# The second expert loop starts while attention still runs: four pairs of expert tiles between the steps of the last turn and the routing

## The reference

```
x = x + 0.5 * ffn(layernorm(x))
x = x + attention(layernorm(x))
x = x + 0.5 * ffn(layernorm(x))
```

```
p = softmax(xt @ Wr + br);  probs, idx = top_k(p, 2);  probs /= probs.sum
h = layernorm(relu(xt @ W1[e] + b1[e]))        # 128 -> 512
y = layernorm(relu(h @ W2[e] + b2[e]))         # 512 -> 128
out = sum over the two chosen experts of probs * y
```

## Time and profile before

| | |
|---|---|
| time, median of 3 runs | 481.54 us (480.0, 481.54, 481.68) |
| profiled execution, from the first instruction to the last | 480.5 us |
| mean granted clock of TensorE | 0.987 of full speed |
| TensorE busy | 430.7 us, with filler |
| VectorE busy | 351.1 us |
| ScalarE busy | 293.5 us |
| GpSimd busy | 244.9 us |

### The profile page before, as it was taken

The page is one execution under the profiler, slowest core; times in us unless marked ns, Lnnn a source line. Parts: engine busy times, 40 slices in busy tenths (PEclk is TensorE's granted clock), DMA queues, the critical chain, the costliest instruction groups (busy, mean ns, idle before and its releaser), DMA issues.

```text
span 480.5 us, 12115 instructions
## 1 busy us (share of the span) xinstructions
PE 430.7 (90%) x3768; PEld 288.1 (60%) x3769; DVE 351.1 (73%) x1268; ACT 293.5 (61%) x593; POOL 244.9 (51%) x344
## 2 busy tenths in 40 slices
PE   7999999999999977889988889878789999999994
PEld 7653676777765444556555565544436777777743
DVE  5874778787886287868889898764654878878764
ACT  1495776666665155777877878747215666676640
POOL 8684634334401557474765847658431454555440
PEclk9997999999999999999999999999999999999999
DMA  7900144445431110000000001101111111111017
GB/s 233 347 25 28 33 137 144 143 154 198 148 123 66 34 34 22 25 13 12 25 24 24 12 25 37 33 23 40 34 51 45 44 51 56 55 52 48 33 49 243
DMA packets 25855, 35.09 MB, mean 73 GB/s; under 512 B 4282, under 2 KB 18546, under 8 KB 24659
## 3 DMA queue, kind: packets, MB, share of 16 engines
q1 hardware_dynamic: 20866, 24.62, 15.4%
q0 software_dynamic: 4944, 9.90, 7.2%
HBM read 15.45 MB, written 18.24 MB: 70 GB/s over the span
## 4 chain that ended last, share of the span: by engine, by line
DVE 32%; PE 28%; issue 12%; ACT 12%; DMA 6%; POOL 5%; DVEq 4%; SPq 1%; POOLq 0%; ACTq 0%
ACT wide L641 8%; DVE st L1037 6%; DVE mx L1649 4%; DVE yy L1054 3%; DMA yk<-y_scratch,posi 3%; DVE st L1060 3%; DVE yy L1058 2%; PE bank L1409 2%; PE bank L1919 2%; POOL yk L1184 2%; DVEq L1054 2%; PE bank L1470 2%; DVE mv L1065 2%; DMA early<-y_scratch 2%; PE bank L1552 2%
## 5 line engine op out<-in xcount | busy, mean ns | idle before, releaser
L807 PEld LDWEIGHTS bank<-w2c,hT 128*128 128x128 f32 x624 | 74.2, 191 | 24.4 <-issue 23.8
L807 PE MATMUL bank<-w2c,hT 128*128 x624 | 76.7, 276 | 3.4 <-ACT hT L663 1.7
L789 PE MATMUL bank<-w1s,xT 128*128 x156 | 73.8, 594 | 0.6 <-DVE w2c L1805 0.6
L1649 DVE TENSOR_REDUCE mx<-bank 128x4 f32<-128x1024 f32 (+1 forms) x48 | 58.4, 1220 | 10.0 <-PE bank L1440 10.0
L412 POOL DMA_INDIRECT y_scratch<-yo,dest_u x39 | 39.2, 1006 | 50.0 <-ACT yo L656 43.7
L1285 ACT ACTIVATE early<-bank 128x768 f32<-128x768 f32 x64 | 51.9, 814 | 20.5 <-PE bank L1460 20.1
L422 POOL DMA_INDIRECT xgw<-xn_scratch,slot_u x39 | 37.2, 953 | 53.2 <-PE bank L781 44.0
L1037 DVE BATCH_NORM_STATS2 st<-wide 128x6 f32<-128x512 f32 x78 | 50.2, 685 | 17.2 <-ACT wide L641 15.8
L663 ACT COPY hT<-bank 128x1024 f32<-128x1024 f32 (+1 forms) x40 | 39.6, 990 | 24.2 <-PE bank L798 24.2
L798 PE MATMUL bank<-ident,wide 128*128 128x128 f32 x312 | 42.0, 277 | 6.5 <-ACT wide L641 6.4
L1184 POOL DMA_INDIRECT yk<-y_scratch,posi x32 | 31.8, 992 | 22.9 <-issue 6.6
(11 more groups left out here) (341 smaller groups left out, 912.1 us busy)
## 6 DMA issues: line engine op xcount, KB each, us to landing
xr_scratch<-row_buf SPq DMA_DIRECT2D x8, 1032.0 KB, 4.1
xgw<-xr_scratch SPq DMA_DIRECT2D x39, 64.5 KB, 1.8
y_scratch<-yo SPq DMA_DIRECT2D x19, 128.0 KB, 1.8
w1s<-in_L_ffn_W_dram SPq DMA_DIRECT2D x1, 2048.0 KB, 9.7
early<-y_scratch SPq DMA_DIRECT2D x8, 256.0 KB, 3.8
xn_scratch<-row_buf SPq DMA_DIRECT2D x1, 1024.0 KB, 5.1
out_dram<-xs SPq DMA_DIRECT2D x8, 128.0 KB, 2.3
row_buf<-row_buf SPq DMA_DIRECT2D x6, 128.0 KB, 2.2
```

Of the source, the lines that this page charges most:

```text
L789: last = pe.matmul(bank[1 + 2 * u + j][:], xT[:, u, j, :], w1s[:, bass.ds(e * FF, FF)], start=True, stop=True)
L807: last = pe.matmul(bank[7][:, j * DIM:(j + 1) * DIM], hT[:, u, j, c * P:(c + 1) * P], w2c[:, bass.ds(e * (FC * DIM) + c * DIM, DIM)], star ...
L1649: dve.tensor_reduce(mx[:, c:c + 2 * per].rearrange("p (a q) -> p q a", q=2), quad[:, low:low + 2, :].rearrange("p q (a e) -> p q a e", a=p ...
```

## The change

The first four pairs of f2 no longer stand in or ahead of the loop. They are written out by hand among the steps of what was turn 10 and the routing of batches 6 and 7. The attention pipeline now ends after turn 9, and its last steps (D of batch 7) stand in this section. For this there are three tile tables in place of one (`tile_table(..., q)`): the first, in turn 9, gives 8 tiles filled from the rows of batches 0 to 3; the second gives 12 from batches 0 to 6; the third the other 19. A table takes only tiles that are full, and carries what it used to the next (`used`, `stride`, `first_at`). `load_tiles` waits for the table and for the scatters of its own row tiles. The filler between these steps is gone, and so are two loads of ScalarE's function table: the exponential of the gates is a power on GpSimd behind the fifth outgoing pair. `gates`, its transpose (`turn_gates`) and its copy (`gates_turned`) stand between the loop and the last four pairs. Within f2 the hidden products of all pairs use one pair of banks (3, 4), so `hidden(m)` waits for relu of m-1.

```diff
+AHEAD = 4
+TABLES = (0, 2 * AHEAD, 20, SLOT_TILES)
...
+            for q in range(3):
+                load_tiles(sp, S, q)
...
+        def load_tiles(sp, S, q):
+            a, b = TABLES[q], TABLES[q + 1]
+            where = lambda n: sp.value_load(addr[0:1, n:n + 1], min_val=0, max_val=(NE * TT + NE - 2) * P)
+            sp.wait_ge(S["slot"], q + 1)
+            first = [where(n) for n in range(a, a + 4)]
+            sp.wait_ge(*scattered(q))
+            for n in range(a, b):
+                p = n // 2
+                v = first[n - a] if n < a + 4 else where(n)
+                if p >= 2:
+                    sp.wait_ge(S["xTp"], p - 1)
+                    sp.wait_ge(S["dest"], p - 1)
+                sp.dma_start(xgw[:, n % 4, :], xr_dram[bass.ds(v, P), :]).then_inc(S[f"xg{n % 4}"], 16)
+        SCATTERED_BY = (0, 8, 14, TT)
+        def scattered(q):
+            semaphore, rows_before = (first_row(0, 0), first_row(0, 1), (sems["f2"]["sc"], 0))[q]
+            return semaphore, rows_before + 16 * TOPK * (SCATTERED_BY[q + 1] - SCATTERED_BY[q])
...
+                pool.wait_ge(S["base"], 3)
+                numbers(0)
+                numbers(1)
+                scatter(pool, S, 12)
+                scatter(pool, S, 13)
+                numbers(2)
+                outgoing(0)
+                numbers(3)
+                scatter(pool, S, 14)
+                scatter(pool, S, 15)
+                numbers(4)
+                for p in range(1, PAIRS):
+                    outgoing(p)
                     if p + 4 < PAIRS:
                         numbers(p + 4)
+                    if p == 4:
+                        pool.wait_ge(S["top"], 1)
+                        pool.tensor_tensor(gden[:], euler[:], mw[:], ALU.pow).then_inc(S["gexp"], 1)
...
+        def pair_banks(S):
+            return (bank[0], (1, 3)) if S is sems["f1"] else (bank[2], (3, 3))
...
-                turn_batch(pe, S, BATCH - 1)
-                keep_warm(1, 6)
-                batch_logits(pe, S, BATCH - 1)
-                keep_warm(4, 6)
-                batch_ranks(pe, S, BATCH - 1)
-                pe.wait_ge(S["base"], 7)
-                pe.matmul(bank[5][:, 0:NE], ones16[:], picks[:, BATCH, 0, :], start=True, stop=True).then_inc(S["rankp"], 1)
-                keep_warm(30, 6)
...
+                if h_at[0] == h_at[1]:
+                    if not (isinstance(m, int) and m == 0):
+                        pe.wait_ge(S["relu"], m)
...
+            def turn_gates():
+                pe.wait_ge(S["gsum"], 1)
+                pe.transpose(gates_bank(first), gsum[:], ident[:]).then_inc(S["gTp"], 1)
...
+                step.settle()
             step(dve.tensor_scalar(one(ntile_i), one(ntile_i), 7, None, ALU.arith_shift_right))
-            step(dve.tensor_tensor(one(ntile), one(ntile_i), picks[0:1, 0, 0, :], ALU.subtract))
+            step(dve.tensor_tensor(one(ntile), one(ntile_i), used[:, 0:NE], ALU.subtract))
+            step.begin(dve.tensor_tensor(stride[:], stride[:], one(ntile), ALU.subtract))
             step(dve.tensor_tensor(one(tri), one(e_lt), ntile[0:1, None, :].to_broadcast([1, NE, NE]), ALU.mult))
...
+            shape = [1, n, NE]
+            step(dve.tensor_tensor(ecmp[:, 0:n], tile_iota[0:1, 0:n, None].to_broadcast(shape), end[0:1, None, :].to_broadcast(shape), ALU.is_ge))
+            step.begin(dve.tensor_reduce(eidf[:, a:b], ecmp[:, 0:n], X, ALU.add))
+            gaps = ecmp[:, 24:24 + n]
+            step(dve.tensor_tensor(gaps, ecmp[:, 0:n], stride[:, None, :].to_broadcast(shape), ALU.mult))
+            begun = lg[0:1].rearrange("p a b -> p (a b)")[:, 0:n]
+            step(dve.tensor_reduce(begun, gaps, X, ALU.add))
+            dve.scalar_tensor_tensor(addr[:, a:b], begun, float(P), first_at[:, 0:n], ALU.mult, ALU.add).then_inc(S["slot"], 1)
+            pack_experts(dve, S, step, a, b)
+            if final:
+                dve.tensor_tensor(mw[:], best8[:, :, 1], best8[:, :, 0], ALU.subtract).then_inc(S["top"], 1)
+                return
+            step(dve.tensor_scalar(one(start), one(start), float(n), None, ALU.min))
+            step(dve.scalar_tensor_tensor(one(end), one(end), float(n), one(start), ALU.min, ALU.subtract))
+            step(dve.tensor_tensor(used[:, 0:NE], used[:, 0:NE], one(end), ALU.add))
+            dve.wait_ge(S["slot"], q + 1)
+            step.begin(dve.tensor_tensor(stride[:], used[:, 1:NE + 1], used[:, 0:NE], ALU.subtract))
+            step(dve.tensor_scalar(first_at[:], tile_iota[0:1, 0:40], used[:, 0:1], float(P), ALU.add, ALU.mult))
...
-            with dve.Fori(1, PAIRS // 2 - 2) as i:
...
+            with dve.Fori(1 if first else AHEAD // 2, PAIRS // 2 - 2) as i:
...
+            if not first:
+                gates(dve, S, step)
...
+            d = BATCH - 1
+            act.activation(spad, eps_c[:], ACT.Sqrt)
+            deviations(act, F, d - 1)
+            half_values(1, d)
+            relu(0, 0)
+            copy_xT(1, 1)
+            turned_batch(act, F, d - 1)
+            copy_hT(0, 0)
+            squares(d)
+            relu(1, 1)
+            act.wait_ge(A["msq"], BATCH)
+            act.activation(orr[:], oms[:], ACT.Sqrt).then_inc(A["rms"], 1)
+            sqrt1(0, 0)
+            copy_xT(2, 0)
+            outputs_turned(d, bank[1])
+            copy_hT(1, 1)
+            relu(2, 0)
+            deviations(act, F, d)
+            sqrt2(0, 0)
+            sqrt1(1, 1)
+            turned_batch(act, F, d)
+            finish(0, 0)
+            copy_xT(3, 1)
+            copy_hT(2, 0)
+            relu(3, 1)
+            sqrt2(1, 1)
+            sqrt1(2, 0)
+            finish(1, 1)
+            copy_hT(3, 1)
+            copy_xT(4, 0)
+            sqrt1(3, 1)
+            sqrt2(2, 0)
+            relu(4, 0)
+            copy_xT(5, 1)
+            finish(2, 0)
...
+            d, e = BATCH - 1, experts(pe, eid, 0, 2 * AHEAD)
+            hidden(0, 0, e[0:2])
+            turn_values(d)
+            pe.wait_ge(A["x2"], d)
+            turn_batch(pe, F, d - 1)
+            turn_x(1, 0, 1)
+            turn_h(0, 0)
+            pe.wait_ge(A["ow"], d + 1)
+            batch_logits(pe, F, d - 1)
+            hidden(1, 1, e[2:4])
+            pe.wait_ge(F["xnTc"], d)
+            second(0, 0, e[0:2])
+            turn_outputs(d, bank[1])
+            batch_ranks(pe, F, d - 1)
+            turn_h(1, 1)
+            turn_x(2, 1, 0)
+            output_products(d, bank[1])
+            hidden(2, 0, e[4:6])
+            second(1, 1, e[2:4])
+            turn_batch(pe, F, d)
+            turn_x(3, 1, 1)
+            turn_h(2, 0)
+            batch_logits(pe, F, d)
+            hidden(3, 1, e[6:8])
+            second(2, 0, e[4:6])
+            batch_ranks(pe, F, d)
+            turn_h(3, 1)
+            pe.wait_ge(F["eid"], 2)
+            later = experts(pe, eid, 2 * AHEAD, 2)
+            turn_x(4, 2, 0)
+            second(3, 1, e[6:8])
+            hidden(4, 0, later)
+            turn_x(5, 2, 1)
...
+                if t == BATCH + 1:
+                    tile_table(dve, F, step, 0)
...
+            d, e = BATCH - 1, experts(dve, eid, 0, 2 * AHEAD - 2)
+            d_step.start(d * D_STEPS)
+            dve.wait_ge(A["x2"], d)
+            row_stats(dve, F, 2 * d - 2, 2 * d)
+            late_norm(dve, F, step, d - 1)
+            weigh(d)
+            outputs(d)
+            stats1(0, 0)
+            mean_squares(d)
+            batch_best(dve, F, step, d - 1)
+            batch_places(dve, F, step, d - 1)
+            rms(d)
+            moments1(0, 0)
+            batch_marks(dve, F, step, d - 1)
+            batch_slots(dve, F, step, d - 1)
+            stats1(1, 1)
+            residual(d, bank[1])
             dve.wait_ge(A["x2"], BATCH)
+            row_stats(dve, F, 2 * d, TT)
+            y_part(0, 0, e[0:2])
+            late_norm(dve, F, step, d)
+            y_norm(0, 0, e[0:2])
+            moments1(1, 1)
+            tile_table(dve, F, step, 1)
+            batch_best(dve, F, step, d)
+            batch_places(dve, F, step, d)
+            batch_marks(dve, F, step, d)
+            y_part(1, 1, e[2:4])
+            batch_slots(dve, F, step, d)
+            stats1(2, 0)
+            y_norm(1, 1, e[2:4])
+            moments1(2, 0)
+            tile_table(dve, F, step, 2)
+            stats1(3, 1)
+            y_part(2, 0, e[4:6])
+            moments1(3, 1)
+            y_norm(2, 0, e[4:6])
+            stats1(4, 0)

```

More of the change, by code:

```diff
@@ L811, in body @@
+            if first:
+                turn_gates()
+            pe.wait_ge(S["eid"], 1 if first else 3)
+            turn_x, hidden, turn_h, second = tensor_pair(pe, S)
             def body(n, i, u, e, kx=2, kh=2, k=2):
@@ L1165, in turns @@
         def turns(eng, turn):
-            for t in range(BATCH + 3):
+            for t in range(BATCH + 2):
                 turn(t, t % 2)
@@ L1532, in turn @@
                         turn8(k6, 0, bank[2][:]).then_inc(A["kTp"], 1)
```

(3 more changed lines are left out.)

411 lines of the change are left out of this document (197 added, 214 removed).

## The result

The changed kernel takes 486.06 us (median of 8 runs, 483.64 to 488.94), the kernel before 482.53 on the same chip (8 runs, 480.00 to 484.11): a ratio of 1.0074, 95% interval 1.0045 to 1.0103. It is slower, by 3.5 us, where 480.1 was predicted, with a range of 475.8 to 484.0. The profiled execution of the changed kernel has a span of 481.9 us and a run time of 483.64, the shortest of the eight.

A forecast was written before the change was run, and what follows sets the result against it. VectorE with ScalarE was taken to bound the loop, behind a single chain across engines. 6.6 us gained before the loop, less 2.5 at the gates and 2.7 for the clock, gave 480.1 us from 481.5; range 475.8 to 484.0.

The forecast's parts named there:

- Tables of 3.9, 3.9 and 3.5 us: VectorE's three new tile tables: forecast working times, with bounds of 3.4 and 4.5 us.
- 4.92 us a pair: Loop of f2: the period of the VectorE and ScalarE ring stays 4.92 us up to pair 15.
- tiles hidden: Tile loads for the first pairs and pair 4 are ready before they are wanted, so they cost nothing.
- 1.6 comes through: Turn 9: the first table makes weigh 2.6 us late, a scatter hides 1.0, and the turn ends 1.6 late.
- The section's sum: VectorE's queue from turn 9 to pair 4's statistics: attention and routing 9.6, pairs 13.4, tables 7.3, waits 10.9 us.
- Its long wait: End of the section: TensorE has nothing to do for 6.6 us before second(3).
- the fall of the clock in it: TensorE's clock is low when second(3) comes, slowing it and hidden(4): 2.7 us lost; this case had chance 0.38.
- the slower rival: Clock falls already in the wait before second(2), stays low into pair 5: 7.4 us lost, 484.8 us, chance 0.20.
- a loss of 2.5: At the gates, now in the loop's ring: one period of 7.4 us in place of 4.92, so 2.5 lost.
- The chain of 7.4 us: From the end of relu(16): statistics, gates, transpose, turn_h, turn_x, hidden, relu, together 7.4 us.
- The forecast of 3.9 gained up to pair 4: From the statistics of batch 5 to those of pair 4, the change was to gain 3.9 us.

The follow-up runs named there:

- h2: Changed kernel with gates moved ahead of pair 17's statistics, 10 filler products in turn 9's wait, 28 ahead of second(3): 477.91 us, ratio 0.9904 to the kernel before.
- e3: Changed kernel with filler at the gates alone, 12 products ahead of their transpose and 2 behind it: ratio 0.9977 to the kernel before.
- e2: Changed kernel with 10 filler products in turn 9 alone, ahead of TensorE's wait for ow: ratio 0.9992 to the kernel before.
- h3: Kernel before with 21 small unused VectorE steps ahead of weigh in turn 9, nothing else changed: ratio 1.0109 to the kernel before.
- h4: Kernel before with 21 small unused VectorE steps ahead of weigh in turn 9 and 10 filler products in TensorE's wait: ratio 1.0050 to the kernel before.
- e4: Changed kernel with 28 filler products ahead of second(3) alone: ratio 0.9886 to the kernel before.
- e1: Changed kernel with filler products in TensorE's three new waits (turn 9, ahead of second(3), at the gates): ratio 0.9914 to the kernel before.

## Why the prediction was wrong

- **Tables of 3.9, 3.9 and 3.5 us; 4.92 us a pair; tiles hidden**: right (4.1, 3.8, 3.4; 4.92; no DMA wait on TensorE). The working of the first two tables, followed from 4.96, gives 4.1 and 4.2, so their 3.9 is not its result.
- **"1.6 comes through"** in turn 9: wrong, 4.5. Two parts. With a full clock it is 2.1 (13.39 in h2, against 11.30): `weigh` is 2.9 us late in place of 2.6, and the power on GpSimd begins 1.8 later. The other 2.4 (15.83 against 13.39; e3 against e2 2.4, h3 against h4 2.1) come from the clock. This step failed since I priced the wait of TensorE that the late `weigh` makes as lateness alone.
- **The section's sum**, 41.2 us of VectorE's queue and 2.7 of the clock; counted from the residual to pair 4 that is 44.1: right to 0.1 us (44.2). Most single waits came as forecast too: 3.4 ahead of `weigh` (3.7), 1.0 for the root (1.0), 1.0 for the projection (0.9), 1.25 for the ranks of batch 7 (1.1). Its long wait (6.6 forecast, 7.19 measured) and the fall of the clock in it are in the profile; that the fall costs 2.7 was shown by e4 and e1 (2.66). Two slips did not matter: turn 9 ends at 334.8 by the text and the sum starts from 334.6, and VectorE is not "mostly idle" in the 27 us ahead of the first hidden products but busy for 15.4.
- **The place before `second(2)`**, the slower rival: the wait is there (2.57) but the clock stayed at 1.00. The loss came out at 3.5 us, the 3.3 of that rival, by another way, so the number agrees and the mechanism does not.
- **"a loss of 2.5"** at the gates: wrong, 4.6. The chain of 7.4 us makes TensorE wait 3.00 and 0.56 us, and `turn_h` and `hidden` behind it ran at half clock. With filler the period is 7.9; so 1.6 is the clock and 0.5 an under-count of the chain.

Most of both errors has one cause. I took the clock into the sum at one wait, the longest, named `second(2)` as a slower case, and summed the waits of turn 9 and of the gates at full clock: 2.4 of the 2.9 us missing in turn 9, and 1.6 of the 2.1 at the gates. The other 0.5 at each are chains sized too short. The forecast of 3.9 gained up to pair 4 less 2.5 became 0.9 less 4.5: -3.6 in place of 1.4.
